# Rows fetched with their weight beside them, and two borders between halves run through: an attention and mixture-of-experts kernel on one core

## What is computed

```python
S = jnp.einsum('bhtd,bhsd->bhts', Q, K)                 # 16 heads of 8 channels
Tm = DEG * jnp.log(jnp.abs(S) + EPS) + jnp.log(scale)   # DEG = 2
Z = Tm + log_G[..., :, None] - log_G[..., None, :]      # causal, gated
y = (exp(Z - max) @ V) / norm
...
_, sel = jax.lax.top_k(scores + expert_bias, 2)         # 8 experts, 2 a token
routed = xf[token_idx] * top_scores_sorted[:, None]
h = jax.nn.silu(routed @ w1[e]) * (routed @ w3[e])      # 128 -> 352 -> 128
out = zeros.at[token_idx].add(h @ w2[e])
```

## Time and profile before

| | |
|---|---|
| time, median of 3 runs | 569.82 us (568.21 to 570.24) |
| profiled execution: time, span | 564.14 us, 562.4 us |
| mean granted TensorE clock | 0.894 |
| PE, DVE, ACT, POOL busy | 79%, 59%, 59%, 55% |
| start to the first unit | 0 to 38 us |
| heads, 80 units | 38 to 217 us |
| jobs of half 0, 1, 2, 3 | 219 to 287, 299 to 375, 389 to 470, 481 to 545 us |
| last returns, adding, storing | 545 to 562 us |

### The profile page before, as it was taken

How to read it: one execution, slowest core, us unless ns; L and a number is a source line. 1 busy time by engine, 2 the same in 40 slices (tenths; PEclk the granted TensorE clock), 3 DMA queues, 4 the chain that set the end, 5 groups by cost and what they waited for, 6 DMA issues and landing times.

```text
span 562.4 us, 11437 instructions
## 1 busy us (share of the span) xinstructions
PE 444.2 (79%) x3822; PEld 328.2 (58%) x3822; DVE 332.3 (59%) x799; ACT 330.5 (59%) x624; POOL 309.6 (55%) x333
## 2 busy tenths in 40 slices
PE   3776998787787786988869989766999677787890
PEld 2554775565565564676646758553777455465670
DVE  5979789959769992425612868364778272131121
ACT  2496799898878676457534655561574463343450
POOL 5344566655652468466464757527557535466641
PEclk9796899989987798989998989985999888699896
DMA  6343461570598202113113111123110222321213
GB/s 151 92 103 72 112 131 21 127 128 7 132 266 170 77 13 59 32 42 75 67 48 99 41 38 36 33 94 117 30 39 29 42 63 70 108 79 43 45 33 126
DMA packets 36371, 43.50 MB, mean 77 GB/s; under 512 B 5876, under 2 KB 31276, under 8 KB 36292
## 3 DMA queue, kind: packets, MB, share of 16 engines
q1 hardware_dynamic: 30428, 30.70, 21.3%
q0 software_dynamic: 5888, 12.07, 8.7%
HBM read 25.91 MB, written 15.86 MB: 74 GB/s over the span
## 4 chain that ended last, share of the span: by engine, by line
PE 50%; DVE 17%; ACT 10%; issue 10%; another core or an unknown queue 6%; DMA 5%; SPq 2%; POOL 1%; ACTq 0%; POOLq 0%; DVEq 0%
PE ps L1578 10%; PE ps L1594 9%; PE ps L1581 9%; DVE A L1026 5%; PE ps L1544 4%; ACT PP L1097 3%; PE ps L1548 2%; PE ps L971 2%; ACT E L1106 2%; PE ps L925 2%; PE ps L1811 1%; DMA QS<-gates 1%; PE ps L993 1%; PE ps L616 1%
## 5 line engine op out<-in xcount | busy, mean ns | idle before, releaser
L1500 POOL DMA_INDIRECT token_out<-ysb,id_out x92 | 91.1, 990 | 109.2 <-ACT ysb L1659 93.9
L1719 DVE TENSOR_TENSOR hid<-silu,ps 128x352 f32<-128x352 f32 x92 | 47.8, 519 | 136.9 <-PE ps L1581 70.2
L1144 POOL TENSOR_TENSOR PP<-PP,E 128x512 f32<-128x512 f32 x64 | 83.1, 1298 | 73.3 <-ACT PP L1097 73.1
L1492 POOL DMA_INDIRECT tiled<-scaled_rows,id_in x92 | 92.1, 1001 | 26.9 <-issue 22.8
L1026 DVE TENSOR_SCALAR A<-ps 128x1024 int32<-128x1024 int32 x80 | 96.1, 1219 | 16.4 <-PE ps L925 15.0
L1097 ACT ACTIVATE PP<-A,feps 128x1024 f32<-128x1024 f32 x80 | 93.1, 1164 | 17.2 <-DVE A L1026 17.0
L1560 ACT ACTIVATE turned<-ps 128x512 f32<-128x512 f32 (+2 forms) x104 | 56.9, 547 | 71.7 <-PE ps L1548 47.5
L1594 PE MATMUL ps<-room,turned 128*128 x552 | 81.1, 285 | 16.1 <-ACT ysb L1659 14.0
L1578 PE MATMUL ps<-room,turned 128*128 x184 | 79.0, 513 | 18.6 <-ACT silu L1652 13.2
L1594 PEld LDWEIGHTS ps<-room,turned 128*128 128x128 f32 x552 | 71.8, 198 | 19.0 <-issue 18.9
L1581 PE MATMUL ps<-room,turned 128*128 x184 | 75.6, 495 | 0.0
(11 more groups left out here) (223 smaller groups left out, 647.9 us busy)
## 6 DMA issues: line engine op xcount, KB each, us to landing
parts<-room SPq DMA_DIRECT2D x32, 128.0 KB, 2.4
scaled_rows<-xT SPq DMA_DIRECT2D x8, 512.0 KB
yb<-token_out SPq DMA_DIRECT2D x8, 512.0 KB
QS<-parts SPq DMA_DIRECT2D x21, 192.0 KB
KS<-parts SPq DMA_DIRECT2D x21, 192.0 KB
room<-in_L_ffn_w_dram SPq DMA_DIRECT2D x2, 1408.0 KB, 8.2
tiled<-scaled_rows,id_in POOLq DMA_INDIRECT x92
token_out<-ysb,id_out POOLq DMA_INDIRECT x92
```

The costliest lines, as they stand in the source:

```text
L1144: g.tensor_tensor(w, w, E[:, hh % 4, :], MUL).then_inc(s_PD, 1)
L1492: g.indirect_dma_start(rows[:, J % ROWS, :], None, xs_d[m], bass.IndirectOffsetOnAxis(ap=id_in[:, m % 2, s:s + 1], axis=0)).then_inc(s_row ...
L1500: g.indirect_dma_start(yr_d[m], bass.IndirectOffsetOnAxis(ap=id_out[:, m % 2, s:s + 1], axis=0), ysb[:, J % OUTS, :], None).then_inc(s_ret ...
```

## The change

1. **Rows with their weight.** `scale_scalar` and its places in the tables are gone. xh gets a 129th column; `weigh` writes the first choice's weight there, one DMA stores the 8 tiles with it, then a new stage `swap` on VectorE waits for that DMA, copies the second choice's weight into the column, and a second DMA stores the same tiles again. The gather fetches 129 numbers a row (516 bytes). The SiLU takes the column as its scale, and the multiplication becomes one of three operands with the column. The gather's wait for its buffer becomes one for `mix_vector` of J - 12, not for the turn. The waits of `turn_scalar` for the stores are gone, and the second layer's normalization gets one.
2. **Two borders run through** (`BEHIND`): halves 1 and 3 follow their forerunner with no drain and no fill. The last two steps of half 0 (and 2) turn the first rows of half 1 (and 3), and the last job of half 0 (and 2) loads the first expert of the next.
3. **Absolute values on ScalarE** for units 4, 65, 71 and 74; the sums of group 14 are taken out by VectorE at unit 79.
4. **Tables**: pieces move between units or slots.

```diff
+        def abs_done(engine, U):
+            if U in ABS_BY_SCALAR:
+                engine.wait_ge(s_Aa, len([n for n in ABS_BY_SCALAR if n <= U]))
+            else:
+                engine.wait_ge(s_A, U + 1 - len([n for n in ABS_BY_SCALAR if n < U]))
...
+        TAKEN_BY_VECTOR = (14,)
+        AT_TAKE_VECTOR = 9
+        ABS_BY_SCALAR = (4, 65, 71, 74)
-        FRONT = {... 'differences': 6, ...}
+        FRONT = {... 'differences': 8, ...}
-        COMBINED_LATE = (61, 66, 71)
...
         def square_scalar(G, p):
-            a.wait_ge(s_A, U + 1)
+            if U in ABS_BY_SCALAR:
+                a.wait_ge(s_S, U + 1)
+                if U >= 3:
+                    a.wait_ge(s_Q, U - 2)
+                bank = BK_S + 2 * (U % 2)
+                a.activation(A[:, U % 3, :], ps[:, bank:bank + 2, :].rearrange("p k t -> p (k t)"), ACT.Abs).then_inc(s_Aa, 1)
+            abs_done(a, U)
...
-                v.tensor_reduce(wts[:], Q16[:], AX.X, ADD).then_inc(s_wts, 1)
+                v.tensor_reduce(wts[:], Q16[:, 1], AX.X, ADD).then_inc(s_wts, 1)
+                v.tensor_reduce(xhw[:, HT * hf:HT * hf + HT, C], Q16[:, 0], AX.X, ADD).then_inc(s_scaled, 1)
...
+            if stage == "swap":
+                v.wait_ge(s_xs, 32 * m + 16)
+                v.tensor_copy(xhw[:, HT * hf:HT * hf + HT, C], wts[:]).then_inc(s_scaled, 1)
...
-                sp.dma_start(flat[:, TB * k:TB * k + TB], xs[:, TB * k:TB * k + TB]).then_inc(s_xs, 16)
+                sp.dma_start(flat[:, :, k, :], xhw[:, HT * (m % 2):HT * (m % 2) + HT, :]).then_inc(s_xs, 16)
...
-                g.wait_ge(s_tp, turns(J - ROWS))
+                g.wait_ge(s_hid, J - ROWS + 1)
...
+        BEHIND = (1, 3)
...
+        def hid_turned(m, t):
+            return t - 1 < JOBS and (t >= 1 or m in BEHIND)
+        def row_turned(m, t):
+            return t + 2 < JOBS or m + 1 in BEHIND
...
-            if s == 0:
+            if s == 0 and m not in BEHIND:
                 pe.wait_ge(s_job, m + 1)
                 turn_tensor_step(m, -2)
...
-            if s == JOBS - 1:
+            if s == JOBS - 1 and m + 1 not in BEHIND:
                 turn_tensor_step(m, JOBS)
                 down_tensor(J - 1)
                 down_tensor(J)
...
-            a.activation(silu[:, J % 2, :], ps[:, BK_A, 0:HID], ACT.Silu).then_inc(s_silu, 1)
+            a.activation(silu[:, J % 2, :], ps[:, BK_A, 0:HID], ACT.Silu, scale=rows[:, J % ROWS, C:CW]).then_inc(s_silu, 1)
...
-            v.tensor_tensor(hid[:, J % 2, 0:HID], silu[:, J % 2, :], ps[:, BK_B + J % 2, 0:HID], MUL).then_inc(s_hid, 1)
+            v.scalar_tensor_tensor(hid[:, J % 2, 0:HID], silu[:, J % 2, :], rows[:, J % ROWS, C:CW], ps[:, BK_B + J % 2, 0:HID],
+                                   MUL, MUL).then_inc(s_hid, 1)
...
-            return (J - ROWS, max(15 + s // 2, J - 8), max(45, J - 8), max(64 + s // 2, J - 9))[m]
+            return (J - ROWS, max(15 + s // 2, J - 8), max(45, J - 8), max(63 + s // 2, J - 9))[m]
```

More of the change, by code:

```diff
@@ L31 @@
 ROWS, OUTS = 12, 8
+CW = C + 1
 LN_EPS = 1e-5
@@ L381, in build @@
         s_A = sem("s_A")
+        s_Aa = sem("s_Aa")
         s_Q = sem("s_Q")
@@ L1020, in heads_vector @@
             for U in range(LAST):
-                if U < PAIRS * GROUPS:
+                if U < PAIRS * GROUPS and U not in ABS_BY_SCALAR:
                     v.wait_ge(s_S, U + 1)
@@ L1108, in take_sums_scalar @@
         def take_sums_scalar(G):
+            if G in TAKEN_BY_VECTOR:
+                return
             a = nc.scalar
@@ L1429, in prepare_vector @@
                 v.tensor_copy(job_expert[:, hf, :], jobf[:, :]).then_inc(s_job, 1)
-        VECTOR_STAGES = ("softmax", "top", "first", "second", "weigh", "slots", "spread", "spread2", "lanes0", "lanes1", "ids", "experts")
+        VECTOR_STAGES = ("softmax", "top", "first", "second", "weigh", "slots", "spread", "spread2", "swap", "lanes0", "lanes1", "ids", "experts")
         def prepare_heads_tensor(U):
@@ L1448, in prepare_heads_scalar @@
                     norm_scalar(b, IN_HEADS[f"apply{b}"].index(U))
-            for k in range(2):
-                if exp and U == IN_HEADS[f"scale{k}"]:
-                    scale_scalar(0, k)
             for b in range(3):
@@ L1526, in steps @@
         def steps(m, t):
-            return (JOBS + 3) * m + t + 3
+            before = sum(JOBS + 3 - 2 * (n in BEHIND) - (n + 1 in BEHIND) for n in range(m))
+            return before + t + 3 - 2 * (m in BEHIND)
         def turns(J):
@@ L1602, in job_tensor @@
                 pe.wait_ge(s_ww, 16 * 5)
-                pe.wait_ge(s_A, PAIRS * GROUPS)
+                for U in range(PAIRS * GROUPS - 3, PAIRS * GROUPS):
+                    abs_done(pe, U)
                 pe.wait_ge(s_E, GROUPS * GH)
-            if s == 0:
+            if s == 0 and m not in BEHIND:
                 pe.wait_ge(s_job, m + 1)
@@ L1691, in between_scalar @@
                         silu_in_scalar(b)
-                    if s == at["turn x"][k]:
+                    if s == at["taken x"][k]:
                         turn_scalar(2, b, BK_X)
@@ L1699, in between_scalar @@
                         squares_scalar(b)
-                    if s == at["turn y"][k]:
+                    if s == at["taken y"][k]:
                         turn_scalar(3, b, BK_X)
```

114 lines of the change are left out of this document (56 added, 58 removed).

## The result

The changed kernel takes 560.73 us (median of 4 runs, 558.55 to 561.59) and the kernel before 569.37 beside it (568.21 to 570.24): ratio 0.984, interval 0.981 to 0.988. It is faster by 8.6 us, not by 31. The time lies above the forecast range (526 to 557), though on the forecast side. The two profiled executions are only 2.7 us apart (561.48 and 564.14), for that of before lies 5.7 us under the median of 569.82 and that of the changed kernel lies close to its own. Why, the runs do not show.

A forecast was written before the change was run, and what follows sets the result against it. The prediction saw no engine full overall, TensorE pacing undisturbed jobs and the pipeline empty at borders. Gains of 34.2 us less 3 of costs gave -31.2, so 539 us on the 569.82 median, range 526 to 557.

The forecast's parts named there:

- First units, routing and end of the heads: Ahead of job 0: absolute values leave VectorE (-2.0 and -3.0 us); VectorE takes group 14's sums, ending TensorE's wait (-0.9).
- Scaling in the halves: Jobs of halves 0, 1 and 2: time lost where ScalarE scales rows comes back, -3.5, -3.2 and -2.0 us.
- Border 0 to 1: Half 0 to half 1 without drain: 9.8 us go, less VectorE's 1.6 us wait for yb, -8.3 us.
- case 3: Chain from half 0's last return through add, mixer and routing paces half 1 and takes the border's gain: 550 us, 20%.
- Border 2 to 3: Half 2 to half 3 without drain: 12.3 us go, less one for late rows, -11.3 us.
- case 6: GpSimd becomes the bound if 129-column gathers cost it more, from 1.65 us each; at 2.2, 588 us; 8%.
- Border 1 to 2: Half 1 to half 2: last step, routing on VectorE, `id_in`, gather and first turn stay the same, no gain.
- Costs: Dearer operands on ScalarE and VectorE, mostly hidden: +3 us (0 to +15.1); gathers of 129 columns and `swap` 0.
- case 4: Both operands, ScalarE's and VectorE's, cost in full: +12.1 us, 551 us, 8%.
- case 2: Gathered rows land later, on the path at jobs 0, 46 and 69: +2.8 us, 541 us, 9%.

The follow-up runs named there:

- 517 us chip: Chip of the first two experiment groups, without "remote" waits: kernel before 518.31 us, changed kernel 508.52 us on the second such chip.
- stalling chips: Chips of the other three experiment groups and the profiled pair, every trace with "remote" waits: the kernel before took 563 to 571 us.
- clean chip: Another name for a chip where the kernel before took 517 us and no trace has a "remote" wait.
- the pair above: Changed kernel with only the border from half 0 to half 1 run through, 508.87 us, and with both borders drained, 508.85 us.

## Why the prediction was wrong

**First units, routing and end of the heads (-5.9).** Right in its sum up to job 0, which comes 6.5 us earlier in the profiled pair and 5.0 on the 517 us chip, where undoing two of the edits alone costs 6 us of time. How it divides among the three terms no run shows. On stalling chips 2.4 to 2.9 us of it are gone by job 2.

**Scaling in the halves (-3.5, -3.2, -2.0).** About right in the first two on the clean chip: -2.5 from job 0 to 22, -3.0 from 42 to 45. In half 2 no gain is seen (+0.3), in a stretch that spreads by 2.5 us; why, the runs do not show.

**Border 0 to 1 (-8.3).** This step failed twice. First in size: I took the whole 12.09 us of the earlier trace rows for the pipeline that drains. On the 517 us chip the same border takes 6.04, so running through can give 3.8 and not 9.8; in the profiled execution three waits put down to "remote" (2.00, 1.17 and 2.35 us) stand in that gap. Then in what the gain meets. My 4 us from job 24's SiLU to the last return were near (4.4 in the changed kernel on the clean chip), but I compared them with a return of before that the stalls had delayed. Without stalls the return comes 2.1 us earlier against job 0 (66.2 and 68.3), about what the scaling had cost half 0, and by the pair above the border adds nothing to it: GpSimd's 2.57 us a job set it before and after. The loads of yb land 4.2 us after their issue, not 2.7, and VectorE waits 3.0 us (3.2 in the pair), not 1.6. The gain was gone by job 30. This was my case 3, at 20%, and its sign was there, 81.2 us for half 1 against 75.8. I priced it at 550, with a return 2.2 us earlier and the other border at nearly its full value.

**Border 2 to 3 (-11.3).** Failed. I wrote that nothing hangs between the jobs there but the ids. Three things do: GpSimd's gathers and returns, the first gather behind the second store, and the adding of half 2's results. The stretch 67 to 69 gave 2.8 us on the clean chip, 69 to 91 gave back 1.3, and undoing the run-through gives the same time. I had the numbers, 2.55 us a job against TensorE's 2.29, and used them only as a mean over all 89 jobs (case 6), where they look harmless at 3.22. The bound lies in a stage, and there GpSimd was full without any dearer gather. The 12.3 us were too large as well: from job 68 to 71 pass 9.9 us in the kernel before without stalls, not the 19.16 of the earlier trace rows, so at most 3.1 could go.

**Border 1 to 2 "stays the same".** Failed: +4.1 to +4.6 us. I asked of `swap` only how long VectorE would wait for the first store (0, right), not who waits for the second. The gather does. And it then ran into the loads of yb, which the earlier last return had moved to the same moment. I had also noted that stores might take over 5 us, and named VectorE and the routing as the ones to pay; the first gather paid.

**Costs (+3).** The operands cost nothing that the times show; ScalarE's +92 ns and VectorE's +59 ns were as priced. Gathers of 129 columns 0, as priced. So case 4 and case 6 as priced are out, and case 2 as well: at the border to half 2, rows of 516 bytes were turned as soon after their gather as those of 512. The Trainium skill, page "DMA: Bandwidth & Descriptors", section "How a descriptor splits into AXI transactions", says that a read off a 256-byte boundary also fetches bytes that it does not use; no time for it is seen here.

Why the changed kernel gains 8.6 us in the medians with its traces 2.7 and 5.5 apart is not settled; in both cases the traced execution of before is a quick one of its kind. On the stalling chips no run undoes a border, so what it is worth there is not measured.

## What to carry to other kernels

When a stage's pipeline is made to run through, compare the paces of all engines in that stage, not over the program: an engine that needs 2.57 us a job beside one that needs 2.29 is hidden only as long as the border lets it catch up, and then it takes the gain. Before calling a gain the border's, see in which stretch of the two traces it lies. For each new store ask who waits for its landing, and for each event that moves earlier, which transfer it now meets. And before costing a gap from one trace, look for waits with no known releaser in it: that part is not the pipeline's.

## What the runs showed of the hardware

The kernel before took 517 (twice), 563, 565, 569 and 571 us (medians) in the groups of runs. In the traces of the slow ones engines wait with no known releaser ("remote"), nearly always for results of TensorE: 59 us in all in the kernel before and 67 in the changed one, the longest 12.2 and 9.1 us; in the traces of the 517 us chips there is no such wait. TensorE's mean granted clock is lower with them (0.894, and 0.939 without, for the kernel before). GpSimd issues a gather and a return every 2.57 us in gapless stretches, with rows of 512 as with rows of 516 bytes. The same steps of TensorE took 2.30 us at a granted clock of 1.00 and 4.21 at 0.55. A store of 516 KB in runs of 516 bytes held its waiter for 5.8 us from its issue (345.97 to 351.76; 5.2 in the profiled trace), where 512 KB in runs of 4 KB moved in 2.66. With two loads of 512 KB issued at the moment of a gather, the first use of its rows came 2.0 to 2.5 us later (5.52 against 3.53; 5.21 against 2.66 with the loads held back).
